# Two-layer graph network: third dense stage with one output of normalised rows and their root, last stage that gathers from it

## The chip, the cores and the metric

The kernel runs on one core of a Trainium2 chip. A core has five engines that work side by side: PE (matrix products; PEld is its weight load), DVE (vector), ACT (scalar, activations), POOL (general; it also issues indirect DMAs) and SP (issues DMAs), and 16 DMA engines that move data between HBM and the on-chip memory. The metric is device time in microseconds (us) of one execution; less is better.

## The reference

50,000 nodes with 256 features each, 12,500 edges sorted by destination. Cut to what matters:

```python
# first layer
e    = gelu((x[src] + edge_attr) @ W_pre + b_pre) * bases
y    = x + segment_sum(e, dst)
h    = relu(bn(y @ W1 + b1));  h = relu(bn(h @ W2 + b2))      # statistics over all nodes
x1   = layernorm(x + y + h)
# second layer
S    = x1[src]
m    = relu(relu(S @ W_rel[r].T + b_rel[r]) @ W_rel[r].T + b_rel[r])   # r = edge type
agg  = segment_sum(m, dst)
i, f, g, o = split(agg @ W_ih.T + b_ih + b_hh)
hn   = sigmoid(o) * tanh(sigmoid(i) * tanh(g))
z    = relu(relu(hn @ M1.T + b1) @ M2.T + b2) @ M3.T + b3
out  = layernorm(x1 + z)
```

A node that is no edge's destination has agg = 0, so its z is one constant row, `base`. Its output is layernorm(x1 + base).

## The kernel before

The program runs five stages one after another, each in a block of its own with a barrier behind it.

`edges0` computes the edge messages of the first layer, 25 blocks of 512 edges, while ACT's queue copies x to the scratch tensor y (25 pieces of 2 MB). After the last block it computes `base` and the bias rows of the second layer in one serial chain (lines 298 to 317 on PE, 358 to 366 on ACT, 444 to 482 on DVE). `dense1` adds the sums to y by indirect DMA and does the first product over 98 blocks of 512 nodes; `dense2` does the second.

`dense3` (line 871) goes over the 98 blocks of nodes once more. For block k: SP loads h2 and y (512 KB each; `load_h2`, `load_y`). ACT's `relu` makes r from h2. PE's `turn` transposes r into PSUM, eight times 128x128. DVE's `add` makes s = 2y + r; `row_stats` (line 857) and `bn_aggr` give mean and variance of each row. POOL's `deviations` (L1016 to L1027) turns variances into 1/root by a power. x1 = (s - mean) / root is made half on DVE (`normed`, L1059), half on ACT (`x1_part`, L1000). POOL's `add_base` (L1034) makes u = x1 + base, DVE takes its statistics too, and ACT's `normed` (L991) writes the normalised o. SP stores x1 and o, 512 KB each. The order on each engine is written out by hand in its `step(k, q)`: DVE does `add(k+3)`, statistics of u(k), `normed(k+1)`, statistics of s(k+3), `bn_aggr` of both; POOL `add_base(k+1)`, then `deviations` for s(k+3) and u(k) in one batch; ACT `x1_part(k+1)`, `relu(k+4)`, `normed(k-1)`. Engines run their instructions in order, and a wait holds up all that stands behind it on the same engine.

```python
def step(k, q):                        # ACT, L1004
    x1_part(k + 1, (q + 1) % 4)
    relu(k + 4, q)
    normed(k - 1, (q - 1) % 4)
```

`edges1` (line 1091) does the second layer for the 25 blocks of 512 edges. POOL fetches x1[src] and x1[dst] by indirect DMA, four of 128 rows to a block each (`fetch_src`, `fetch_dst`, L1190, L1200), and stores the new rows of a block into out (`store`, L1219, four). PE does the products in an order written out over k (L1310 on); in step k DVE makes u(k-1) and its statistics, POOL's `deviations(k-1)` follow. At its start SP loads the marks `cont` (1.6 MB) and `has` (3.2 MB), broadcast to all partitions.

Of the kernel before, what the change touches and what calls it, by code (L numbers as in the profile page):

```python
# [15 lines left out]
F = 256  # L16
C = F // P
# [9 lines left out]
COLS = 40  # L27
# [79 lines left out]
def edges0(nc, A, K, S):  # L107


    with ExitStack() as c:  # L110
# [5 lines left out]
        def sem(name):  # L116
# [10 lines left out]
        spare = [attr[:, (S.EB + n) % 4].rearrange("p c e -> p (c e)") for n in range(3)]  # L127
        raw_m = spare[0][:, 0:(NBLK - M1) * P].rearrange("p (n o) -> p n o", o=P)
        raw_rel = spare[1].rearrange("p (r c o) -> p r c o", r=2, c=C)
        rows = spare[2][0:4, 0:2 * F].rearrange("p (n f) -> p n f", n=2)  # L130
        spare_bases = bases[:, S.EB % 3].rearrange("p c e -> p (c e)")
        rows_h = spare_bases[0:4, 0:2 * F].rearrange("p (n f) -> p n f", n=2)
        rows_l = spare_bases[0:4, 2 * F:4 * F].rearrange("p (n f) -> p n f", n=2)
        wm_h, wm_l = sb("wm_h", [P, NBLK - M1, P], F32R), sb("wm_l", [P, NBLK - M1, P], F32R)
# [13 lines left out]
        hid_h, hid_l = sb("hid_h", [P, C, P], F32R), sb("hid_l", [P, C, P], F32R)  # L148
        a1, a1h, a1l = sb("a1", [P, P]), sb("a1h", [P, P], F32R), sb("a1l", [P, P], F32R)
# [8 lines left out]
        rel_i_full, has_done, has_kept, rel_full, bias_product = (  # L158
            sem("e0_rel_i_full"), sem("e0_has"), sem("e0_has_kept"), sem("e0_rel_full"), sem("e0_bias_product"))
# [9 lines left out]
        biases, cell_done, hid_done, gates_on, mlp_done, relu_done, product = (  # L169
            sem("e0_biases"), sem("e0_cell"), sem("e0_hid"), sem("e0_gates_on"), sem("e0_mlp"), sem("e0_relu"),  # L170
            sem("e0_product"))
        block = c.enter_context(nc.Block())
        EB = S.EB

        @block.sync
        def _(sp):
# [30 lines left out]
            sp.dma_start(K.b3[:], A["M_b3"].rearrange("(a f) -> a f", a=1).to_broadcast([P, F])).then_inc(wm_full, 16)  # L207
# [13 lines left out]
            sp.wait_ge(lo_done, EB - 3)  # L221
            sp.dma_start(raw_m, A["wt"][:, M1:NBLK]).then_inc(wm_full, 16)
            sp.wait_ge(lo_done, EB - 2)
            sp.dma_start(raw_rel.rearrange("p r c o -> p (r c o)"), A["wt"][:, REL:IH].rearrange("p b o -> p (b o)")).then_inc(rel_full, 16)
            sp.wait_ge(lo_done, EB - 1)
            sp.dma_start(rows, A["rows"]).then_inc(wm_full, 16)
# [30 lines left out]
        def _(pe):  # L257
# [29 lines left out]

            pe.wait_ge(consts, 1)
# [3 lines left out]
            for k in range(EB + 1):  # L292
                if k + 2 < EB:
                    turn(k + 2)
                if k < EB:
                    dense(k)
                if k >= 1:
                    back(k - 1)

            pe.wait_ge(gelu_done, EB)  # L300
            pe.wait_ge(rel_full, 16)
            pe.wait_ge(cols_full, 16)
            for r in range(2):
                for ic in range(C):
                    last = pe.matmul(pU[0:4, 1, r * F:(r + 1) * F], K.rel_b4[:, ic],
                                     raw_rel[:, r, ic], start=ic == 0, stop=ic == C - 1)
            last.then_inc(bias_product, 1)
            pe.wait_ge(mlp_done, 1)
            for ic in range(C):
                last = mm3(pe, pU[:, 0, 0:P], (wm_h[:, ic], wm_l[:, ic]), (hid_h[:, ic], hid_l[:, ic]), ic == 0, ic == C - 1)  # L310
            last.then_inc(product, 1)
            pe.wait_ge(mlp_done, 2)
            mm3(pe, pU[:, 0, 0:P], (wm_h[:, M2 - M1], wm_l[:, M2 - M1]), (a1h[:], a1l[:]), True, True).then_inc(product, 1)
            pe.wait_ge(mlp_done, 3)
            w3_h, w3_l = (w[:, M3 - M1:M3 - M1 + C].rearrange("p b o -> p (b o)") for w in (wm_h, wm_l))
            mm3(pe, pU[:, 0, 0:F], (a1h[:], a1l[:]), (w3_h, w3_l), True, True).then_inc(product, 1)

        @block.scalar
        def _(act):
# [37 lines left out]

            act.wait_ge(biases, 1)
            for n, func in ((0, ACT.Sigmoid), (1, ACT.Tanh), (2, ACT.Sigmoid)):
                act.activation(gate[:, n], K.gate_b[:, n * C:(n + 1) * C], func).then_inc(gates_on, 1)  # L360
            act.wait_ge(cell_done, 1)
            act.activation(cell_t[:], cell[:], ACT.Tanh).then_inc(gates_on, 1)
            act.wait_ge(product, 1)
            act.activation(a1[:], pU[:, 0, 0:P], ACT.Relu, bias=K.m_b[:, 0:1]).then_inc(relu_done, 1)
            act.wait_ge(product, 2)
            act.activation(a1[:], pU[:, 0, 0:P], ACT.Relu, bias=K.m_b[:, 1:2]).then_inc(relu_done, 1)

        @block.vector
        def _(dve):
# [36 lines left out]

            dve.wait_ge(run_full, 32)
# [9 lines left out]
            dve.wait_ge(consts, 5)  # L417
            dve.wait_ge(index_full, 48)
# [25 lines left out]

            dve.wait_ge(cols_full, 16)
            dve.tensor_tensor(out=K.gate_b[:], in0=K.cols[:, 0:GATES * C], in1=K.cols[:, GATES * C:2 * GATES * C],
                              op=ALU.add).then_inc(biases, 1)
            dve.wait_ge(wm_full, 48)
            then(dve.tensor_copy(wm_h[:], raw_m))
            then(dve.tensor_tensor(out=wm_l[:], in0=raw_m, in1=wm_h[:].bitcast(F32), op=ALU.subtract))  # L450
            dve.tensor_scalar(out=K.minus_rel_b[:], in0=K.rel_b, scalar1=-1.0, scalar2=None, op0=ALU.mult)
            dve.memset(K.ones[:].bitcast(F32), 1.0)
            then(dve.memset(K.rows[:].bitcast(F32), 0.0))
            then(dve.tensor_scalar(out=keep_l[:], in0=K.part[0:4], scalar1=2.0, scalar2=None, op0=ALU.is_ge))
            then(dve.tensor_scalar(out=keep_h[:], in0=K.part[0:4], scalar1=2.0, scalar2=None, op0=ALU.is_lt))
            then(dve.tensor_scalar(out=odd[:], in0=keep_l[:], scalar1=-2.0, scalar2=K.part[0:4, 0:1],
                                   op0=ALU.mult, op1=ALU.add))
            then(dve.tensor_scalar(out=even[:], in0=odd[:], scalar1=-1.0, scalar2=1.0, op0=ALU.mult, op1=ALU.add))
            dve.wait_ge(bias_product, 1)
            for r, mark in ((0, even), (1, odd)):  # L460
                then(dve.scalar_tensor_tensor(out=rows[:, 0], in0=pU[0:4, 1, r * F:(r + 1) * F], scalar=mark[:, 0:1],
                                              in1=rows[:, 0], op0=ALU.mult, op1=ALU.add))
            then(dve.tensor_copy(rows_h.bitcast(F32R), rows))
            then(dve.tensor_tensor(out=rows_l, in0=rows, in1=rows_h, op=ALU.subtract))
            then(dve.tensor_scalar(out=rows_l, in0=rows_l, scalar1=keep_l[:, 0:1], scalar2=None, op0=ALU.mult))
            for n in range(2):
                then(dve.scalar_tensor_tensor(out=K.rows[0:4, n], in0=rows_h[:, n], scalar=keep_h[:, 0:1],
                                              in1=rows_l[:, n], op0=ALU.mult, op1=ALU.add))
            dve.wait_ge(gates_on, 3)
            dve.tensor_tensor(out=cell[:], in0=gate[:, 0], in1=gate[:, 1], op=ALU.mult).then_inc(cell_done, 1)  # L470
            dve.wait_ge(gates_on, 4)
            dve.tensor_tensor(out=hid[:], in0=gate[:, 2], in1=cell_t[:], op=ALU.mult).then_inc(hid_done, 1)
            dve.wait_ge(hid_done, 1)
            wide = hid[:].rearrange("p (c o) -> p c o", o=1).to_broadcast([P, C, P])
            then(dve.tensor_copy(hid_h[:], wide))
            dve.tensor_tensor(out=hid_l[:], in0=wide, in1=hid_h[:].bitcast(F32), op=ALU.subtract).then_inc(mlp_done, 1)
            for n in range(2):
                dve.wait_ge(relu_done, n + 1)
                then(dve.tensor_copy(a1h[:], a1[:]))
                dve.tensor_tensor(out=a1l[:], in0=a1[:], in1=a1h[:].bitcast(F32), op=ALU.subtract).then_inc(mlp_done, 1)  # L480
            dve.wait_ge(product, 3)
            then(dve.tensor_tensor(out=K.base[:], in0=pU[:, 0, 0:F], in1=K.b3[:], op=ALU.add))
# [1153 lines left out]
```

## Time and profile before

| | |
|---|---|
| median of 3 runs | 2237.25 us (2236.58 to 2238.08) |
| profiled execution | 2248.79 us, of which its span is 2247.0 |
| `edges0` | 0 to about 302 us |
| `dense1` and `dense2` | about 304 to 1042 us |
| `dense3` | 1042 to 1582 us |
| `edges1` | 1583 to 2247 us |
| busy, whole span | PE 72%, DVE 74%, ACT 61%, POOL 58% |
| moved | 572.69 MB |

The page's second part cuts the span into 40 slices of 56 us; a digit is the busy share in tenths, and PEclk the clock granted to PE in tenths of full speed (2.4 GHz; 5 is 1.2 GHz). The stages are told apart by which engine is busy in them and by which lines the timeline shows. The profiled execution took 11.5 us more than the median of the timed runs.

### The profile page before, as it was taken

The page shows a single profiled execution, that of the slowest core. Times are in us where ns is not written, and L with a number is a line of the kernel's source. Part 1 is how long each engine was busy: PE and PEld are TensorE (multiplying, and loading weights), DVE is VectorE, ACT ScalarE, POOL GpSimd, SP SyncE. Part 2 cuts the span into 40 slices and gives each one's busy share as a digit, 9 for nine tenths or more (in the row PEclk, how much of TensorE's full clock was granted, in tenths as well). Part 3 has the DMA queues.
Part 4 walks back from the last instruction along what each step waited for, and adds up shares of the span by engine and source line. Part 5 has one row for each costly group of instructions (what it writes and reads, how often), then busy time and mean ns, then how long its engine had stood idle before and what let it go on. Part 6 is the DMA issues. An engine that isn't in the chain of part 4 may idle for free. (4 is left out here: it accounts for less than half of the span.)

```text
span 2247.0 us, 29418 instructions
## 1 busy us (share of the span) xinstructions
PE 1609.5 (72%) x7554; PEld 1295.5 (58%) x7554; DVE 1666.1 (74%) x3358; ACT 1365.9 (61%) x1981; POOL 1313.1 (58%) x1204
## 2 busy tenths in 40 slices
PE   2645569999996888994333333332599999999994
PEld 2434448888884655663232233232488778888884
DVE  2646646666667888996999999998377667777673
ACT  1322325555775766773888888887266656666663
POOL 5543147770006887001999999999446666666653
PEclk8877879999998999997555555555799999999997
DMA  9999759998879999995999999997412111212110
GB/s 341 368 347 352 260 161 340 342 340 316 289 249 285 342 339 342 344 325 232 385 397 399 401 404 400 395 407 308 169 37 67 63 62 57 65 63 64 55 53 32
DMA packets 171831, 572.69 MB, mean 255 GB/s; under 512 B 27441, under 2 KB 50583, under 8 KB 170322
## 3 DMA queue, kind: packets, MB, share of 16 engines
q1 hardware_dynamic: 123282, 445.99, 52.3%
q0 software_dynamic: 47136, 73.04, 13.8%
q10 hardware_dynamic: 1344, 52.84, 6.3%
q8 instruction: 31, 0.51, 0.1%
q14 instruction: 38, 0.31, 0.0%
HBM read 332.27 MB, written 295.04 MB: 279 GB/s over the span
## 5 line engine op out<-in xcount | busy, mean ns | idle before, releaser
L968 PE MATMUL d_pN<-k_ident,d_r 128*128 128x128 f32 x784 | 191.6, 425 | 337.2 <-ACT d_r L983 336.5
L968 PEld LDWEIGHTS d_pN<-k_ident,d_r 128*128 128x128 f32 x784 | 153.0, 222 | 375.9 <-issue 343.9
L500 DVE BATCH_NORM_STATS2 k_stats<-d_pH 128x512 f32 (+1 forms) x392 | 253.2, 688 | 100.8 <-PE d_pH L52 91.7
L991 ACT ACTIVATE d_o<-d_u,d_nb,d_rs 128x256 f32<-128x256 f32 x392 | 203.6, 590 | 81.2 <-POOL d_nb L1027 81.2
L1034 POOL TENSOR_TENSOR d_u<-d_x,k_base 128x1024 f32<-128x1024 f32 x98 | 230.9, 2356 | 14.6 <-DVE d_x L1059 9.5
L590 POOL DMA_INDIRECT scratch_y<-k_sums,k_target x98 | 151.9, 1550 | 120.7 <-POOLq L61 69.1
L50 PE MATMUL d_pH<-d_r_h,k_w_h 128*128 128x512 f32 x392 | 164.3, 419 | 57.3 <-DVE d_r_l L829 27.5
L780 ACT ACTIVATE d_r<-d_h,d_coef 128x512 f32<-128x512 f32 x196 | 149.2, 809 | 87.0 <-DVE d_r_l L829 41.8
L637 ACT ACTIVATE d_y_h<-d_pT 128x1024 fp32r<-128x1024 f32 x98 | 100.5, 1025 | 157.2 <-PE d_pT L606 133.1
L811 POOL DMA_INDIRECT scratch_y<-k_sums,k_target x98 | 175.0, 1786 | 33.3 <-issue 21.8
L530 POOL TENSOR_TENSOR bn_rstd<-bn_var,k_minus_half 128x2 f32<-128x2 f32 x2 | 1.5, 726 | 318.3 <-DMA d_h<-scratch_h 176.7
L237 POOL DMA_INDIRECT edge<-in_x,k_src x100 | 116.1, 1161 | 116.8 <-PE pT L264 89.7
L1025 POOL TENSOR_TENSOR d_rs<-d_v,k_minus_half 128x8 f32<-128x8 f32 (+1 forms) x101 | 166.2, 1645 | 8.4
L50 PE MATMUL d_pH<-d_y_h,k_w_h 128*128 128x512 f32 x392 | 163.4, 417 | 0.0
L676 DVE TENSOR_TENSOR d_y_l<-d_pT,d_y_h 128x1024 fp32r<-128x1024 f32 x98 | 120.0, 1225 | 57.7 <-ACT d_y_h L637 52.5
L983 ACT ACTIVATE d_r<-d_h,k_coef 128x512 f32<-128x512 f32 x196 | 147.5, 800 | 21.9 <-DMA d_h<-scratch_h 21.9
L1200 POOL DMA_INDIRECT e_xd<-scratch_x,k_dst_gather x98 | 144.6, 1476 | 26.6 <-issue 26.6
L52 PE MATMUL d_pH<-d_r_h,k_w_l 128*128 128x512 f32 x392 | 154.9, 395 | 0.0
L51 PE MATMUL d_pH<-d_r_l,k_w_h 128*128 128x512 f32 x392 | 154.4, 394 | 0.0
L52 PE MATMUL d_pH<-d_y_h,k_w_l 128*128 128x512 f32 x392 | 154.2, 393 | 0.0
L51 PE MATMUL d_pH<-d_y_l,k_w_h 128*128 128x512 f32 x392 | 153.3, 391 | 0.0
L1372 ACT ACTIVATE e_gate<-pG,k_gate_b 128x512 f32<-128x512 f32 (+1 forms) x150 | 99.1, 674 | 87.8 <-PE pG L52 65.1
(201 smaller groups left out, 4960.1 us busy)
## 6 DMA issues: line engine op xcount, KB each, us to landing
d_y<-scratch_y SPq DMA_DIRECT2D x196, 512.0 KB
scratch_h<-d_h SPq DMA_DIRECT2D x196, 512.0 KB
d_h<-scratch_h SPq DMA_DIRECT2D x196, 512.0 KB
scratch_y<-in_x ACTq DMA_DIRECT2D x25, 2000.0 KB
scratch_x<-d_x SPq DMA_DIRECT2D x97, 512.0 KB
out<-d_o SPq DMA_DIRECT2D x97, 512.0 KB, 7.7
attr<-in_attr_t SPq DMA_DIRECT2D x25, 512.0 KB, 28.4
bases<-in_bases_t SPq DMA_DIRECT2D x25, 512.0 KB
```

The lines of the kernel that those rows point to most:

```text
L50: pe.matmul(out, lhs[0], rhs[0], start=first, stop=False)
L51: pe.matmul(out, lhs[0], rhs[1], start=False, stop=False)
L52: return pe.matmul(out, lhs[1], rhs[0], start=False, stop=last)
L500: return dve.bn_stats(out, psum)
L590: pool.indirect_dma_start(out=A["y"], out_offset=bass.IndirectOffsetOnAxis(ap=K.target[:, t:t + 1], axis=0), in_=K.sums[:, t], in_offset=N ...
L780: last = act.activation(r[:, q % 2, cc], h1[:, q, cc * B:(cc + 1) * B], ACT.Relu, bias=coef[:, 1, cc:cc + 1], scale=coef[:, 0, cc:cc + 1])
L811: pool.indirect_dma_start(out=A["y"], out_offset=bass.IndirectOffsetOnAxis(ap=K.target[:, k:k + 1], axis=0), in_=K.sums[:, k], in_offset=N ...
L968: last = pe.transpose(pN[b][:, j, cc * P:(cc + 1) * P], r[:, b, cc, j * P:(j + 1) * P], K.ident[:])
L983: last = act.activation(r[:, q % 2, cc], h2[:, q, cc * B:(cc + 1) * B], ACT.Relu, bias=K.coef2[:, 1, cc:cc + 1], scale=K.coef2[:, 0, cc:cc ...
L991: last = act.activation(o[:, q, j], u[:, q, j], ACT.Identity, bias=nb[:, q, J + j:J + j + 1], scale=rs[:, q, J + j:J + j + 1])
L1025: pool.tensor_tensor(out=rs[:, q, now], in0=v[:, q, now], in1=K.minus_half[:, now], op=ALU.pow).then_inc(rs_done, 1)
L1034: pool.tensor_tensor(out=u[:, q], in0=x1[:, q], in1=wide, op=ALU.add).then_inc(u_done, 1)
```

## The change

`dense3` has one output for each block instead of two: rows of 260 columns, of which 256 are the normalised row and the next is its root sqrt(var + eps). x1 is not stored; it is root times the row, up to the mean of x1 + base, which is taken into the biases. The statistics of two rows come from one `bn_stats` over 512 elements read in turn from the two rows, with no `bn_aggr`. s is summed in PSUM by PE: a float32 product of y with twice the identity and eight products of r with the identity. DVE makes u = s / root + base out of PSUM, four rows of 256 columns. SP's store of block k follows the load of block k+7. ACT's order is new: `relu(0..3)`, then `normed(k)`, `relu(k+4)` for each k.

`edges1` gathers from out. Because its own stores overwrite rows that are still to be read as sources, blocks 0 to 3 of the sources are fetched directly, and blocks 4 to 24 are fetched in steps -1 to 5, three blocks a step, into `bounce`, moved out by SP to a scratch tensor and loaded from there later. Stores are held until step 6 (six buffers of o), then go three blocks a step until they have caught up. DVE multiplies source rows by their root (four instructions a block). `has` is loaded block by block. The chain at the end of `edges0` that makes `base` moves into its steps 5 to 10, with products of four columns, and its weights are loaded earlier.

```diff
 # edges0
-            sp.wait_ge(lo_done, EB - 3)
-            sp.dma_start(raw_m, A["wt"][:, M1:NBLK]).then_inc(wm_full, 16)
...
+                if SIDE <= k < SIDE + 5:
+                    base_mlp(k - SIDE)
...
+                if k == SIDE - 1:
+                    base_row()
+                if SIDE <= k < SIDE + 5:
+                    dve.wait_ge(side_product, k - SIDE + 1)
+                    (first_mlp, second_mlp, third_mlp, shifted_biases, bias_rows)[k - SIDE]()
 # dense3, SP
+            for k in range(NB + 3):
+                if k + 4 < NB:
+                    load(k + 4)
+                if k >= 3:
+                    store(k - 3)
 # dense3, PE
+            for k in range(NB):
+                pe.wait_ge(y_full[k % 4], 16 * (k // 4 + 1))
+                if k >= 4:
+                    pe.wait_ge(u_done, k - 3)
+                for two in range(J // 2):
+                    pe.matmul(pN[k % 4][:, 2 * two:2 * two + 2].rearrange("p j f -> p (j f)"), twice[:],
+                              y[:, k % 4, two * 2 * F:(two + 1) * 2 * F], start=True, stop=False)
                 pe.wait_ge(relu_done, k + 1)
-                wait(pe, s_done, k - 1)
                 for j in range(J):
                     for cc in range(C):
-                        last = pe.transpose(pN[b][:, j, cc * P:(cc + 1) * P], r[:, b, cc, j * P:(j + 1) * P], K.ident[:])
-                last.then_inc(turned, 1)
+                        last = pe.matmul(pN[k % 4][:, j, cc * P:(cc + 1) * P], r[:, k % 2, cc, j * P:(j + 1) * P], K.ident[:],
+                                         start=False, stop=j % 2 == 1 and cc == C - 1)
+                last.then_inc(summed, 1)
 # dense3, ACT
+            def normed(k):
+                n = (k - 1) % 4
+                act.wait_ge(nb_done, k + 1)
+                act.wait_ge(u_done, k + 1)
...
+            for k in range(4):
+                relu(k)
+            for k in range(NB):
+                normed(k)
+                if k + 4 < NB:
+                    relu(k + 4)
 # dense3, POOL
+            for n in range(-3, NB - 1):
+                a, b, at = n + 3, n + 1, n % 4
+                if real(a):
+                    pool.wait_ge(st1_done, a + 1)
+                if real(b):
+                    pool.wait_ge(st2_done, b + 1)
...
+                pool.tensor_scalar(out=v[:, at, now], in0=st[:, at, now, 2], scalar1=1.0 / F, scalar2=EPS,
+                                   op0=ALU.mult, op1=ALU.add).then_inc(v_done, 1)
...
+                pool.tensor_tensor(out=rs[:, at, now], in0=v[:, at, now], in1=K.minus_half[:, now], op=ALU.pow).then_inc(rs_done, 1)
...
+                    pool.tensor_tensor(out=nb[:, at], in0=nm[:, at], in1=rs[:, at, J:2 * J], op=ALU.mult).then_inc(nb_done, 1)
 # dense3, DVE
+            def pairs(out, rows):
+                for p in range(J // 2):
+                    last = dve.bn_stats(out[:, 2 * p:2 * p + 2].rearrange("p j s -> p (j s)"),
+                                        rows[:, 2 * p:2 * p + 2].rearrange("p j f -> p f j"))
...
+            def first(k):
+                dve.wait_ge(summed, k + 1)
...
+                pairs(st[:, (k - 3) % 4, 0:J], pN[k % 4]).then_inc(st1_done, 1)
+            def second(k):
+                dve.wait_ge(rs_done, batches(k - 3))
...
+                for j in range(J):
+                    last = dve.scalar_tensor_tensor(out=u[:, k % 3, j], in0=pN[k % 4][:, j], scalar=rs[:, (k - 3) % 4, j:j + 1],
+                                                    in1=K.base[:], op0=ALU.mult, op1=ALU.add)
...
+                pairs(st[:, (k - 1) % 4, J:2 * J], u[:, k % 3]).then_inc(st2_done, 1)
+            for k in range(-3, NB - 1):
+                if real(k + 3):
+                    first(k + 3)
+                if real(k + 1):
+                    second(k + 1)
 # edges1, POOL: order of a step
+                for n in now[0:1]:
+                    pick_src(n)
                 if real(k - 1):
                     deviations(k - 1)
                 if real(k + 1):
                     fetch_dst(k + 1)
-                if real(k - 1):
-                    store(k - 1)
-                if 2 <= k + 4 < EB:
-                    fetch_src(k + 4)
+                for n in now[1:]:
+                    pick_src(n)
...
+                if k >= HELD:
+                    for _ in range(3):
+                        if stored < min(k, EB):
+                            store(stored)
+                            stored += 1
 # edges1, DVE
+                    for j in range(tiles(k + 2)):
+                        row = xs[:, b, j]
+                        last = dve.tensor_scalar(out=row[:, 0:F], in0=row[:, 0:F], scalar1=row[:, F:F + 1], scalar2=None,
+                                                 op0=ALU.mult)
+                    last.then_inc(scaled, 1)
```

Here `rs_done` and `batches(n) = n + 4` count POOL's batches from n = -3; `nb_done` counts only batches with a block b, so `nb_done >= k + 1` is the batch n = k - 1.

## Rows read from the trace of the kernel before

**Rows 1.** Page, part 2: the span in 40 slices, busy and clock in tenths.
```profile
DVE  2646646666667888996999999998377667777673
PEclk8877879999998999997555555555799999999997
```

**Rows 2.** Windows: us; busy PE, PEld, DVE, ACT, POOL; clock; DMA share; GB/s.
```profile
800.00:900.00 100.00, 80.81 (x324) 58.44 (x323) 83.81 (x109) 68.70 (x82) 78.72 (x45) 1.00 1.09 342
1200.00:1300.00 100.00, 37.80 (x155) 29.87 (x153) 96.18 (x363) 85.52 (x154) 91.01 (x96) 0.50 1.02 400
2000.00:2100.00 100.00, 99.81 (x481) 83.54 (x479) 70.91 (x100) 62.16 (x92) 67.08 (x66) 1.00 0.21 65
```

**Rows 3.** Timeline, DVE, `dense3`: start, us, line, operation, tiles, count [idle before].
```profile
1300.86 1.18 DVE L1051 SCALAR_TENSOR_TENSOR d_s<-d_y,d_pN 128x1024 f32<-128x1024 f32 x1
1301.96 1.39 DVE L860 BATCH_NORM_STATS2 d_st<-d_u 128x6 f32<-128x256 f32 x4
1303.28 0.72 DVE L1059 TENSOR_SCALAR d_x<-d_s,d_mv,d_rs 128x256 f32<-128x256 f32 x2
1305.45 0.64 DVE L1081 BATCH_NORM_AGGREGATE d_mv<-d_st 128x2 f32<-128x6 f32 x8
1306.01 1.19 DVE L1051 SCALAR_TENSOR_TENSOR d_s<-d_y,d_pN 128x1024 f32<-128x1024 f32 x1
```

**Rows 4.** The same stretch, ACT.
```profile
1304.09 2.08 ACT L991 ACTIVATE d_o<-d_u,d_nb,d_rs 128x256 f32<-128x256 f32 x4 [0.91 <-POOL d_nb L1027]
1306.07 1.08 ACT L1000 ACTIVATE d_x<-d_s,d_nb,d_rs 128x256 f32<-128x256 f32 x2
1307.06 1.51 ACT L983 ACTIVATE d_r<-d_h,k_coef 128x512 f32<-128x512 f32 x2
```

**Rows 5.** The same stretch, POOL.
```profile
1301.44 0.24 POOL L1022 TENSOR_SCALAR d_nm<-d_mv 128x8 f32<-128x8 f32 x1
1302.07 1.67 POOL L1025 TENSOR_TENSOR d_rs<-d_v,k_minus_half 128x8 f32<-128x8 f32 x1
```

**Rows 6.** The same stretch, PE.
```profile
1303.31 1.96 PE L968 MATMUL d_pN<-k_ident,d_r 128*128 128x128 f32 x8 [3.30 <-ACT d_r L983]
```

**Rows 7.** Timeline, DVE: first block and last row statistics of `dense3`.
```profile
1055.34 1.22 DVE L1051 SCALAR_TENSOR_TENSOR d_s<-d_y,d_pN 128x1024 f32<-128x1024 f32 x1
...
1573.87 0.38 DVE L1081 BATCH_NORM_AGGREGATE d_mv<-d_st 128x2 f32<-128x6 f32 x4 [0.15 <-DVE d_st L860]
```

**Rows 8.** Timeline: statistics of 512 columns, float32 products, transposes at full clock.
```profile
287.19 3.58 PE L305 MATMUL pU<-attr,k_cols 128*4 128x256 f32 x8
...
324.19 1.30 DVE L500 BATCH_NORM_STATS2 k_stats<-d_pH 128x6 f32<-128x512 f32 x2 [0.59 <-PE d_pH L52]
...
2003.39 1.03 PE L1247 MATMUL pX<-k_ident,e_xs 128*128 128x128 f32 x8
```

**Rows 9.** Window inside those float32 products, columns as in Rows 2.
```profile
287.00:288.00 1.00, 1.00 (x5) 0.23 (x4) 0.96 (x2) 0.71 (x1) 0.00 (x0) 0.50 0.06 16
```

**Rows 10.** Timeline, end of `edges0`: DVE, ACT, DVE, POOL.
```profile
255.18 1.22 DVE L383 TENSOR_TENSOR attr<-pT,attr 128x1024 f32<-128x1024 f32 x1 [17.50 <-DMA attr<-in_attr_t]
...
287.29 1.02 ACT L342 ACTIVATE k_sums<-pS 128x1024 f32<-128x1024 f32 x1 [4.38 <-PE pS L285]
...
301.59 0.42 DVE L482 TENSOR_TENSOR k_base<-pU,k_b 128x256 f32<-128x256 f32 x1 [1.10 <-PE pU L52]
...
304.06 1.62 POOL L590 DMA_INDIRECT scratch_y<-k_sums,k_target  x1 [69.13 <-POOLq L61]
```

**Rows 11.** Timeline, PE: the first instruction of `edges1`.
```profile
1596.01 1.97 PE L1247 MATMUL pX<-k_ident,e_xs 128*128 128x128 f32 x8 [39.31 <-DMA e_xs<-scratch_x,k_src]
```

**Rows 12.** Groups by line, POOL, 1690 to 2170 us: count | busy us, mean ns.
```profile
L1200 POOL DMA_INDIRECT e_xd<-scratch_x,k_dst_gather x76 | 114.5, 1506 | 20.5 <-issue 20.5
L1219 POOL DMA_INDIRECT out<-e_o,k_target x80 | 84.0, 1050 | 24.4 <-issue 24.4
L1190 POOL DMA_INDIRECT e_xs<-scratch_x,k_src x74 | 79.6, 1076 | 22.6 <-issue 22.6
```

More of the change, by code:

```diff
@@ L16 @@
 F = 256
+FP = 260
 C = F // P
@@ L297, in _ @@
                 if k >= 1:
+                    if SIDE < k <= SIDE + 5:
+                        pe.wait_ge(side_ready, k - SIDE + 1)
                     back(k - 1)
[L300 to L316, printed above, removed]
+                if SIDE <= k < SIDE + 5:
+                    base_mlp(k - SIDE)
         @block.scalar
@@ new lines, in first_mlp, with second_mlp, third_mlp @@
+            def first_mlp():
+                dve.tensor_scalar(out=a1[:], in0=pS[:, 0, 0:4], scalar1=K.m_b[:, 0:1], scalar2=0.0,
+                                  op0=ALU.add, op1=ALU.max).then_inc(side_ready, 1)
+            def second_mlp():
+                dve.tensor_scalar(out=a2[:], in0=pS[:, 0, 0:1].to_broadcast([P, P]), scalar1=K.m_b[:, 1:2], scalar2=0.0,
+                                  op0=ALU.add, op1=ALU.max).then_inc(side_ready, 1)
+            def third_mlp():
+                then(dve.tensor_tensor(out=K.base[:], in0=pS[:, 0], in1=b3[:], op=ALU.add))
+                then(dve.bn_stats(base_st[:], K.base[:]))
+                then(dve.bn_aggr(base_mv[:], base_st[:]))
+                for oc in range(C):
+                    last = dve.tensor_scalar(out=base4[:, oc], in0=pS[:, 1, oc * 4:(oc + 1) * 4], scalar1=K.b3_col[:, oc:oc + 1],
+                                             scalar2=base_mv[:, 0:1], op0=ALU.add, op1=ALU.subtract)
+                last.then_inc(side_ready, 1)
@@ new lines, in shifted_biases @@
+            def shifted_biases():
+                moved = pS[:, 0, 0:2 * C * 4].rearrange("p (n o) -> p n o", o=4)[:, :, 0]
+                then(dve.tensor_tensor(out=K.minus_rel_b[:], in0=moved, in1=K.rel_b, op=ALU.subtract))
+                for r in range(2):
+                    for n in (r, r + 2):
+                        last = dve.tensor_scalar(out=b4[:, :, n], in0=K.minus_rel_b[:, r * C:(r + 1) * C], scalar1=-1.0,
+                                                 scalar2=None, op0=ALU.mult)
+                last.then_inc(side_ready, 1)
@@ L452, in _ @@
[L452 to L480, printed above, removed]
@@ L481, in _ @@
-            dve.wait_ge(product, 3)
-            then(dve.tensor_tensor(out=K.base[:], in0=pU[:, 0, 0:F], in1=K.b3[:], op=ALU.add))
+                if k == SIDE - 1:
+                    base_row()
+                if SIDE <= k < SIDE + 5:
+                    dve.wait_ge(side_product, k - SIDE + 1)
+                    (first_mlp, second_mlp, third_mlp, shifted_biases, bias_rows)[k - SIDE]()
 def node_rows(t, S):
@@ L854, in _ @@
             coef2_vector(dve)
-def row_stats(dve, stats, rows, done):
-    for j in range(J):
-        last = dve.bn_stats(stats[:, j], rows[:, j])
-    last.then_inc(done, 1)
-def row_moments(dve, mv, stats, past, done):
-    dve.sem_inc(past, 1)
-    for j in range(J):
-        last = dve.bn_aggr(mv[:, j], stats[:, j])
-    last.then_inc(done, 1)
 def dense3(nc, A, K, S):
@@ L1004, in step @@
-            def step(k, q):
-                if real(k + 1):
-                    x1_part(k + 1, (q + 1) % 4)
-                if real(k + 4):
-                    relu(k + 4, q)
-                if real(k - 1):
-                    normed(k - 1, (q - 1) % 4)
-            act.dma_start(raw_wl[:], A["wt"]).then_inc(K.wl_full, 16)
-            batch_steps(act, S.NB, step, 4)
+            act.dma_start(raw_wl[:], A["wt"]).then_inc(wl_full, 16)
+            for k in range(4):
+                relu(k)
@@ L1029, in add_base @@
-            def add_base(k, q):
-                pool.wait_ge(x1_done, k + 1)
-                pool.wait_ge(x1_rest, k + 1)
-                wait(pool, o_done, k - 3)
-                wide = K.base[:].rearrange("p (o f) -> p o f", o=1).to_broadcast([P, J, F])
-                pool.tensor_tensor(out=u[:, q], in0=x1[:, q], in1=wide, op=ALU.add).then_inc(u_done, 1)
-            def step(k, q):
-                if real(k + 1):
-                    add_base(k + 1, (q + 1) % 4)
-                if real(k + 3) or real(k):
-                    deviations(k, q)
@@ L1176, in _ @@
             sp.dma_start(cont[:], line.to_broadcast([P, S.TC * P])).then_inc(marks, 16)
[L1177 to L1179 removed]
+            load_has(2)
+            for k in range(-2, EB):
+                if k >= 1 and k + 3 < EB:
+                    load_src(k + 3)
+                if k >= 0 and k + 2 < EB:
+                    load_has_k(k + 2)
+                    if k + 3 < EB:
+                        load_has(k + 3)
+                for n in picks(k):
+                    move_out(n)
         @block.gpsimd
```

471 lines of the change are left out of this document (250 added, 221 removed).

## The prediction

> **What bounds the kernel now.** I read the slices of the page first, to see the stages by the busiest engine and by PE's clock [rows 1]; then one window in each of three stages [rows 2]; then the timeline of one step of `dense3`, engine by engine [rows 3 to 6]. The reader is to see three things. `dense3` runs with DVE at 96% and DMA at 400 GB/s, and PE, 38% busy, at half clock [rows 2]: 2.1 MB a block at 400 GB/s is 5.2 us, and DVE's step from one sum to the next is 5.15 us [rows 3], so two bounds lie together. `edges1` is PE's: 99.8% busy, DVE 71% [rows 2]. `edges0` waits for its loads near its end (17.5 us before the sum at 255) and closes with a serial chain in which no bulk transfer runs: the last sums are kept at 288.3, `base` is ready at 302.0, `dense1`'s first add starts at 304.06 [rows 10].
>
> **dense3, by throughput.** Bytes: 512 + 512 + 520 KB a block, 1.58 MB, 3.95 us at the 400 GB/s of [rows 2]. DVE: four statistics of 512 columns at 1.30 us the pair, 2.6 us [rows 8]; they replace eight of 256 (1.39 us for four [rows 3]), and `bn_aggr` (0.64) goes. The sum of 1024 columns (1.18) and the two scalings (0.72 for two, so the second starts 0.32 after the first) give way to four multiply-adds of 256, 1.36 us by that pitch [rows 3]. With one wait of DVE for itself (0.15 [rows 7]) that is 4.1 us. ACT: 1.98 + 1.51 = 3.5 us [rows 4], as `x1_part` (0.99) goes. POOL: `add_base` goes, 2.65 us from the first of its small operations to ACT's start stay [rows 4, 5]. PE: the eight products with the identity and the two with twice the identity have no row. The nearest is eight float32 products of 256 columns, 0.43 us each (3.58 less an end of about 0.15, by eight) at clock 0.50 [rows 8, 9], which is two clocks a column at 1.2 GHz. So y costs 2 x 0.85 = 1.7 us at that clock, and r 8 x 0.21 = 1.7, in line with the 1.96 that eight transposes take there [rows 6] and with 1.03 at full clock [rows 8]. Bounds for r: 1.03 below, 8 x 0.43 = 3.4 above (its weights have 128 columns, those of the row four). I take 1.96. By throughput alone the block would take 4.1 us, and 1.1 us a block would be won.
>
> **dense3, by its order.** I do not believe that number, because a loop of waits closes within two steps. DVE's step m is `first(m+3)`, then `second(m+1)`. Follow one block: `second(k)` ends step k-1. POOL's batch n = k-1 waits for it. ACT's `normed(k)` waits for that batch, and `relu(k+4)` stands behind `normed(k)` in ACT's queue. PE's r products of k+4 wait for `relu(k+4)`, and `first(k+4)` opens DVE's step k+1. Only step k lies between. The loop takes:
>
> - DVE step: 1.30 + 1.36 + 0.15 + 1.30 = 4.11 [rows 3, 7, 8]
> - to POOL 0.15 (priced as [rows 7]), POOL to ACT's start 1304.09 - 1301.44 = 2.65 [rows 4, 5]; the power stays eight wide, 1.67 of it
> - ACT `normed` 1.98, `relu` 1.51 [rows 4]
> - to PE 0.15, r products 1.96 at half clock [rows 6], to DVE 0.15
>
> That is 12.66 us for two steps, 6.3 us a step, against 5.15 now. Other loops are looser: y's products need only `second(k)`'s multiply-adds and fit into the 2.6 us and more that PE has left over at half clock (6.3 - 3.7); u has three buffers, which makes three steps; loads and stores have four blocks' time. The order of before holds the same loop over three steps: POOL's start at 1301.44, `normed`, `x1_part`, `relu` to 1308.57, then 0.15 and 1.96 give 1310.7 [rows 4 to 6]. With DVE's step and two hops that is 14.6 us, 4.9 a step, just under 5.15. It hid; with one step less it can't.
>
> PE's clock decides 0.47 us of this. PE would be busy for 3.7 of 6.3 us at half clock, 59%, with about 2.6 us idle in a piece. The rows have 38% at 0.50 and 81% at 1.00 [rows 2], so neither side is excluded. I take 0.50, as the work of this stage is next to the row of this stage.
>
> Sum for the stage. DVE's first block is at 1055.3 and its last `bn_aggr` ends at 1574.25 [rows 7]. After: the first four blocks go at PE's pace, 3.7 us, and step 0 ends at about 1055.3 + 11 + 4 = 1070. The other 96 steps take 96 x 6.3 = 605, to 1675. What follows (POOL, ACT, store) is as now. That is +101 us.
>
> **edges0.** The chain behind the last kept sums goes: from 288.3 to 304.06 stand 15.7 us, of which the barrier's 2.05 (302.01 to 304.06) stays, 13.7 us [rows 10]. Against it 0.85 MB of weights now load among the bulk loads, 2.4 us at 350 GB/s (`edges0` moves about what the 342 of [rows 2] shows). The moved steps wait in six blocks for each other (side products, small vector operations, two changes of the ACT table), some 20 us in total as an estimate from the chain's own 13.7 and its new hops; they are covered by the loads, for which DVE stalls 17.5 us at a time [rows 10]. Queued behind the waits are DVE's next sums and, through them, PE. If that cover is gone, up to 20 us come back. I take -11, range -14 to +6.
>
> **edges1.** PE starts at 1596, after the first sources, which share DMA with 4.8 MB of marks [rows 11]. Of these 2.8 MB come later, at most 7 us at 400 GB/s; the scaling of the sources (1.36 and a hop) goes in between. I take -3. In steady state DVE gains 1.36 us of scaling and 0.1 of multiply-adds and loses 0.5 of statistics and aggregation, with 29% free [rows 2]; PE has the same products. I cost it at nothing; were the cover gone, it would be 1 us a step, 24 us. POOL issues 16 DMAs in each of seven steps in place of 12: twelve at 1.08 + 0.30, four at 1.51 + 0.27, and 2.1 for `deviations` make 25.8 us [rows 5, 12], against a step of 24 us (80 stores in 480 us [rows 12]). Behind them wait `deviations` (needed by DVE a step later) and SP's moves. 7 x 1.8 = 13 us of lag meet some 10 us of lead: I take +2, range 0 to +30. The last stores are as now. Together -1.
>
> **Sum.** +101 - 11 - 1 = +89 us, against the profiled execution's 2248.8. That one lies 11.5 us above the median; the difference is applied to the median: 2237.25 + 89 = 2326 us.
>
> **Rivals.**
>
> 1. **PE at full clock in dense3.** r takes 1.03 in place of 1.96, the step 5.84: 96 x 0.47 = 45 us less, 2281. For it: real products, not transposes, and 59% busy. Against: 38% gave 0.50.
> 2. **The float32 products with 128 columns of weights cost double,** 3.4 for r: +1.5 on the loop, +72 us, 2398. [rows 8, 9] speak against it (two clocks a column, but with four columns of weights). The Trainium skill, "FP8 and Floating Point Precision", TensorE Precision Notes, says that true FP32 takes four passes through the array; by that each product would take 0.43 us and the time would be this rival's, while the row shows half of it.
> 3. **Statistics over two rows read in turn run at half rate,** 0.53 us more for each of four: +2.13 on the loop, +102 us, 2428. No row reads with such a stride, so the bound is open upwards. The Trainium skill, "SBUF — State Buffer", section "Door 1: The DMA port swizzle", says that an access that crosses to a new 16-byte line at each element pays a penalty; that would be this rival, and no row here shows it.
> 4. **POOL holds edges1 up.** If all sixteen issues cost 1.5 + 0.30, a step takes 30.9 us, 7 x 6.9 = 48 of lag less some 18 of lead: 28 us above the forecast, 2354.
> 5. **The loop does not bind, and the stage goes by throughput.** If ACT had `relu` far enough ahead, DVE's 4.1 us would be the step: 96 x 2.2 = 211 us less, 2115, faster than before. It decides from 5.2 us a step down: for that the loop would have to be 10.3 us and not 12.7. For it: ACT is only 55% busy by the sum, and bytes fall by a quarter. Against: `relu(k+4)` does stand behind `normed(k)`, and its pieces are measured.
>
> **How the numbers follow.** Forecast 0.47, rival 1 0.17, rival 4 0.10, rival 2 0.08, rival 3 0.10, rival 5 0.08. The range takes in the forecast and rivals 1, 2 and 4, with some 10 us for the small terms: 2268 to 2408. It leaves out 0.18. Only rival 5 is faster. Within 0.2% (4.5 us, about what a measurement of this kernel can tell from no change) lies no case, for mixtures 0.01. So faster 0.08, same 0.01, slower 0.91.
>
> **What would show it.** The step of `dense3`, from one `first` to the next, averages 6.3 us; DMA falls to about 250 GB/s and DVE to about 65% there; DVE waits before `first` for PE, PE before r for ACT's `relu`, ACT before `normed` for POOL. From the end of `second(k)` to the start of `first(k+4)` stand 8.5 us. `dense1` begins at about 293. Step times of 4.1 us, DVE or DMA at the brim, would prove me wrong; statistics of more than 0.7 us, or r products of more than 2.2, would make a rival right. In `edges1` PE stays above 97%.

## The result, and the profile after

The changed kernel takes 2398.68 us (median of 4 runs, 2397.45 to 2402.3) against 2237.58 for the kernel before beside it: 1.0723 times as long, 95% interval 1.0705 to 1.0742. That is 161 us slower, where 89 were forecast. The profiled execution took 2402.3 us with a span of 2400.5; all that follows compares it with the span of 2247.0 before, a difference of 153.5 us. The other 7.6 us are no loss that the profiles could show: the profiled execution before lies 11.2 us above its median, the one after 3.6.

Where the time went, by the same marks in both traces (us; for before, the starts in [rows 7, 10] and the two rows below):

| stretch | before | after | difference | forecast |
|---|---|---|---|---|
| start to first operation of `dense1` | 304.06 | 288.54 | -15.5 | -11 |
| from there to the first sum or statistic of `dense3` | 751.3 | 755.6 | +4.3 | 0 |
| `dense3` on DVE, first to last | 518.9 | 677.3 | +158.4 | +101 |
| to the first `e_xt_l` | 24.8 | 23.1 | -1.7 | -3 |
| `edges1`, from there to the last `e_u` | 629.9 | 638.9 | +9.0 | +2 |
| to the end | 18.1 | 17.2 | -0.9 | 0 |

The marks on DVE, kernel before (timeline: start, us, engine, line, operation, tiles, count [idle before]), first and last of `edges1`:

```profile
1599.07 1.23 DVE L1436 TENSOR_TENSOR e_xt_l<-pX,e_xt_h 128x1024 fp32r<-128x1024 f32 x1 [15.35 <-ACT e_xt_h L1344]
...
2228.94 0.69 DVE L1494 TENSOR_TENSOR e_u<-pM,e_xd 128x512 f32<-128x512 f32 x1 [2.16 <-issue]
```

The same of the changed kernel, with the first and the last statistics of `dense3`:

```profile
1044.09 1.30 DVE L1037 BATCH_NORM_STATS2 d_st<-d_pN 128x6 f32<-128x512 f32 x2 [2.23 <-PE d_pN L969]
...
1720.09 1.30 DVE L1037 BATCH_NORM_STATS2 d_st<-d_u 128x6 f32<-128x512 f32 x2
...
1744.47 1.23 DVE L1485 TENSOR_TENSOR e_xt_l<-pX,e_xt_h 128x1024 fp32r<-128x1024 f32 x1 [3.11 <-ACT e_xt_h L1391]
...
2383.35 0.87 DVE L1553 SCALAR_TENSOR_TENSOR e_u<-e_xd,pM 128x256 f32<-128x256 f32 x2 [2.17 <-PE pM L53]
```

The page of the changed kernel, part 2, the rows that answer to [rows 1]:

```profile
DVE  3674566666678889946556656655457687777873
...
PEclk8886799999989999968878878878689999999996
```

DVE's nines in `dense3` have become fives and sixes, and PE's clock, an even 5 before, is mostly 7 and 8 there. The windows (columns as in Rows 2) of `dense3` and `edges1`:

```profile
1200.00:1300.00 100.00, 68.30 (x289) 49.28 (x290) 57.86 (x112) 50.32 (x87) 34.99 (x73) 0.79 0.67 228
...
2000.00:2200.00 200.00, 200.00 (x957) 167.36 (x956) 156.71 (x214) 127.95 (x188) 105.83 (x103) 1.00 0.24 72
```

Nothing is at its brim in `dense3`: PE 68%, DVE 58%, ACT 50%, POOL 35%, 228 GB/s in place of 400. That is the look of a loop of waits. The page's groups show who waits for whom (count | busy us, mean ns | idle before, its main releaser):

```profile
L969 PE MATMUL d_pN<-k_ident,d_r 128*128 128x128 f32 x1568 | 268.9, 343 | 222.0 <-ACT d_r L980 222.0
...
L991 ACT ACTIVATE d_o<-d_u,d_nb,d_rs 128x256 f32<-128x256 f32 x392 | 203.2, 589 | 340.5 <-POOL d_nb L1026 340.4
...
L1037 DVE BATCH_NORM_STATS2 d_st<-d_pN 128x6 f32<-128x512 f32 x196 | 126.4, 687 | 272.2 <-PE d_pN L969 271.9
```

DVE waits for PE, PE for ACT, and ACT for POOL. That POOL waits for DVE closes the loop; this the profile does not name (it has "issue" ahead of L1018), but the kernel does (`st2_done`), and POOL starts 0.15 us after DVE's statistics end. One turn of it, on the timeline of the changed kernel (DVE, POOL, ACT and PE rows in order of time):

```profile
1301.89 1.29 DVE L1037 BATCH_NORM_STATS2 d_st<-d_pN 128x6 f32<-128x512 f32 x2 [5.41 <-PE d_pN L969]
...
1303.77 1.95 PE L969 MATMUL d_pN<-k_ident,d_r 128*128 128x128 f32 x16
...
1304.78 1.31 DVE L1037 BATCH_NORM_STATS2 d_st<-d_u 128x6 f32<-128x512 f32 x2
...
1305.55 1.88 PE L964 MATMUL d_pN<-d_y,d_twice 128*128 128x512 f32 x4
...
1306.01 1.28 DVE L1037 BATCH_NORM_STATS2 d_st<-d_pN 128x6 f32<-128x512 f32 x2
...
1306.24 0.20 POOL L1018 TENSOR_SCALAR d_v<-d_st 128x8 f32<-128x8 f32 x1 [7.04 <-issue]
...
1308.68 2.07 ACT L991 ACTIVATE d_o<-d_u,d_nb,d_rs 128x256 f32<-128x256 f32 x4 [6.12 <-POOL d_nb L1026]
...
1310.66 1.50 ACT L980 ACTIVATE d_r<-d_h,k_coef 128x512 f32<-128x512 f32 x2
...
1312.22 3.38 PE L969 MATMUL d_pN<-k_ident,d_r 128*128 128x128 f32 x16 [4.78 <-ACT d_r L980]
...
1315.63 1.30 DVE L1037 BATCH_NORM_STATS2 d_st<-d_pN 128x6 f32<-128x512 f32 x2 [5.45 <-PE d_pN L969]
```

`second` ends at 1306.09, POOL's batch starts 0.15 later, `normed` 2.44 after that, `relu` 1.98 later, r's products 1.56 later and take 3.38, and `first` opens the next step but one at 1315.63: 9.54 us, and with DVE's own step of 4.2 the 13.74 us from 1301.89 to 1315.63. Two steps go back to back, then DVE idles 5.4 us. That is the loop of the prediction, over two steps as foreseen. The turn shown has r's products at 3.38 us; over the 38 such turns read between 1100 and 1640 us they take 3.07 to 3.79, on average 3.57. What is new stands in the counts: r's eight products are **sixteen records**, y's two products four. A float32 product leaves two records here.

### The profile page after: what moved, and what is told of

Read it like the earlier page. It is cut to its first block and busy times, and to the rows that moved or that the text cites. A ratio compares the mean times of both kernels' runs of the same rounds, so it can differ in the third digit from the quotient of the medians.

```text
span 2400.5 us, 28831 instructions
## 1 busy us (share of the span) xinstructions
PE 1882.5 (78%) x8746; PEld 1483.1 (62%) x8746; DVE 1606.3 (67%) x2311; ACT 1274.3 (53%) x1785; POOL 1087.8 (45%) x1198
## 5 line engine op out<-in xcount | busy, mean ns | idle before, releaser
L969 PE MATMUL d_pN<-k_ident,d_r 128*128 128x128 f32 x1568 | 268.9, 343 | 222.0 <-ACT d_r L980 222.0
L969 PEld LDWEIGHTS d_pN<-k_ident,d_r 128*128 128x128 f32 x1568 | 256.1, 252 | 287.2 <-ACT d_r L980 261.5
L1037 DVE BATCH_NORM_STATS2 d_st<-d_pN 128x6 f32<-128x512 f32 x196 | 126.4, 687 | 272.2 <-PE d_pN L969 271.9
L964 PE MATMUL d_pN<-d_y,d_twice 128*128 128x512 f32 x392 | 208.6, 658 | 23.3 <-DMA d_y<-scratch_y 23.3
L1018 POOL TENSOR_SCALAR d_v<-d_st 128x8 f32<-128x8 f32 (+1 forms) x100 | 20.0, 200 | 441.8 <-issue 413.6
L1052 DVE SCALAR_TENSOR_TENSOR d_u<-d_pN,d_rs,k_base 128x256 f32<-128x256 f32 x392 | 161.0, 474 | 0.0
```

Source lines behind the costliest of these rows:

```text
L964: pe.matmul(pN[k % 4][:, 2 * two:2 * two + 2].rearrange("p j f -> p (j f)"), twice[:], y[:, k % 4, two * 2 * F:(two + 1) * 2 * F], start=T ...
L969: last = pe.matmul(pN[k % 4][:, j, cc * P:(cc + 1) * P], r[:, k % 2, cc, j * P:(j + 1) * P], K.ident[:], start=False, stop=j % 2 == 1 and ...
L1052: last = dve.scalar_tensor_tensor(out=u[:, k % 3, j], in0=pN[k % 4][:, j], scalar=rs[:, (k - 3) % 4, j:j + 1], in1=K.base[:], op0=ALU.mult ...
```

## The experiments

### Is it the loop, and over how many steps? (relu first)

```diff
             for k in range(NB):
-                normed(k)
                 if k + 4 < NB:
                     relu(k + 4)
+                normed(k)
```

> Against the changed kernel, only the order of two steps on ACT in dense3 differs: relu(k+4) stands ahead of normed(k). Theory (a loop of waits that closes within two of DVE's steps, 13.7 us measured, because relu stands behind normed): the loop now closes over three steps, 4.11 + 0.15 + 2.44 + 1.98 + 1.50 + 0.15 + 3.38 + 0.15 = 13.9 us for three, 4.6 us a step, or 4.2 if PE's clock rises to full (r 1.95); against 6.98 now that is 97 x 2.4 to 97 x 2.8, so 2130 to 2170 us in all, DVE about 95% busy in the stage. Rival (PE's own work bounds the step: eight r products and two y products at half clock would take 3.4 + 3.4 = 6.8 us): nothing changes, 2400 us. A second rival (1.58 MB a block, if the stage could move no more than the 230 GB/s seen): 6.9 us a step, 2400 us.

Measured: 2131.66 us (2128.75 to 2135.76), 0.9534 of the kernel before (0.9517 to 0.955), so 267 us below the changed kernel and 105 below the kernel before. `dense3` takes 410.7 us in place of 677.3. Its window, columns as above:

```profile
1200.00:1300.00 100.00, 91.06 (x488) 59.71 (x487) 99.13 (x195) 84.05 (x145) 58.10 (x122) 1.00 1.01 383
```

DVE is 99% busy with a step of 4.1 us, and 383 GB/s flow. The same products, bytes and statistics run in 0.6 of the time, so neither PE's work nor the transfers held the changed kernel. Two steps on ACT in the other order did. Part of the gain is PE's clock, 1.00 here and 0.79 there: the kernel with y twice (below) has the old order at 1.00, and its `dense3` takes 609.5 us. As an estimate from these, 68 of the 267 us come with the clock and some 199 with the loop's third step.

### One piece of the loop longer, one shorter (power twice, half of r)

```diff
...
+                pool.tensor_tensor(out=more[:, at, now], in0=v[:, at, now], in1=K.minus_half[:, now], op=ALU.pow)
                 pool.tensor_tensor(out=rs[:, at, now], in0=v[:, at, now], in1=K.minus_half[:, now], op=ALU.pow).then_inc(rs_done, 1)
```

> The changed kernel with one more power of the same size on POOL in each batch of dense3, into a tile that nobody reads (1.64 us in the trace). Theory (POOL's batch lies on the loop, and the loop closes within two steps): +1.64 us on 13.74, +0.82 us a step, 97 x 0.82 = +80 us, 2480 us. Rival (PE's work or the transfers bound the step; POOL has 4 of 7 us free): no change, 2400 us. If the loop closed within one step it would be +159, within three +53.

Measured: 2482.42 us, `dense3` 760.4, +83.1. That is 0.85 us for each of 98 blocks, where half of the 1.64 added is 0.82; a loop of one step would give 1.64, of three 0.55. The small rest is not settled: r's products where they bind are 3.74 us long on average here, 0.17 more than before, which alone would be 0.08 a block. POOL, 35% busy, passed half of its added time on: the share that a loop over two steps gives.

```diff
                 for j in range(J):
-                    for cc in range(C):
+                    for cc in range(1):
                         last = pe.matmul(pN[k % 4][:, j, cc * P:(cc + 1) * P], r[:, k % 2, cc, j * P:(j + 1) * P], K.ident[:],
-                                         start=False, stop=j % 2 == 1 and cc == C - 1)
+                                         start=False, stop=j % 2 == 1)
```

This kernel leaves out the second half of r, so its output is not the reference's.

> The changed kernel without the four of eight r products of a block that carry the second half of the features (so the sum lacks r there); all else stays. Theory (r's products are 3.4 us of the two-step loop): -1.7 us on the loop, -0.85 us a step, 97 x 0.85 = -82 us, 2318 us. Rival (PE's work bounds the step): -1.7 us a step, -165 us, 2235 us. If r's products were not on the loop: 2400 us.

Measured: 2313.87 us, `dense3` 602.2, -75.1, 0.77 us a block. A turn that binds has, on PE in this kernel:

```profile
1310.92 1.88 PE L969 MATMUL d_pN<-k_ident,d_r 128*128 128x128 f32 x8 [4.11 <-ACT d_r L980]
```

Over the turns from 1100 to 1640 us the r products that bind take 2.04 us on average, against 3.57 in the changed kernel: 1.53 less, half of it 0.77. The product is on the loop with its full length, and PE's total work isn't what counts (that would have been -1.7 a step).

### The clock of the product on the loop (y twice)

```diff
+                for two in range(J // 2):
+                    pe.matmul(pN[k % 4][:, 2 * two:2 * two + 2].rearrange("p j f -> p (j f)"), twice[:],
+                              y[:, k % 4, two * 2 * F:(two + 1) * 2 * F], start=True, stop=True)
                 for two in range(J // 2):
```

> The changed kernel with the two products of y issued twice in each block of dense3 (each first pair is a closed sum of its own that the second overwrites, so the result is the same): more work for PE, placed where PE waits for ACT's relu. Theory (a loop of two steps, with r's eight products on it at the granted clock; y's products lie beside it): if the added work brings the clock from half during r to full, r takes 1.95 in place of 3.38, -0.72 us a step, about -70 us, 2330 us. If the clock stays at half, PE has 3.4 + 2 x 3.4 = 10.2 us of work a step and the time is about 2700 us. Rival (PE's work bounds the step now): longer in either case, by 97 x 1.7 = 165 us at full clock, 2565 us, or more.

Measured: 2378.43 us, 48 above the theory's 2330 and far below the rival's 2565. Its `dense3` took 609.5 us, 67.8 less than in the changed kernel. Most of the rest lay in `edges1` (678.6 in place of 638.9), and two other kernels on the same chip had the same (below). So it ran again beside the changed kernel:

> The changed kernel with y's products issued twice in dense3, once more beside the changed kernel on one chip. Its dense3 took 609.5 us from the first statistics to the last in place of 677.3. Theory: 68 us less than the changed kernel here, with PE's clock at 1.00 in the stage. Rival (the stage's gain is given back in edges1, as its first run of 2378 us could be read): 20 to 25 us less only.

Measured: 2365.83 against 2432.67 us, -66.8, `dense3` 609.5 against 676.5. A window of `dense3` in this last run:

```profile
1200.00:1300.00 100.00, 86.56 (x392) 52.29 (x392) 66.55 (x128) 55.74 (x96) 39.12 (x81) 1.00 0.75 255
```

And the r products that bind, on its timeline:

```profile
1311.34 2.05 PE L972 MATMUL d_pN<-k_ident,d_r 128*128 128x128 f32 x16 [1.62 <-ACT d_r L983]
```

More work made the kernel faster. In the changed kernel PE idles 4.78 us ahead of the r products that bind, and as they start the clock falls. Windows of 1 us there, columns as above:

```profile
1311.00:1312.00 1.00, 0.00 (x0) 0.00 (x0) 0.00 (x0) 1.00 (x2) 1.00 (x1) 1.00 0.44 166
1312.00:1313.00 1.00, 0.78 (x5) 0.79 (x6) 0.00 (x0) 0.32 (x2) 0.88 (x3) 0.85 0.89 362
1313.00:1314.00 1.00, 1.00 (x7) 1.00 (x6) 0.00 (x0) 1.00 (x3) 0.00 (x0) 0.50 0.71 160
...
1316.00:1317.00 1.00, 1.00 (x3) 0.38 (x2) 1.00 (x3) 0.32 (x1) 0.00 (x0) 0.95 0.50 45
```

So these 3.38 us are for the most part, not all, at 1.2 GHz; in turns where the clock has fallen before they start (below, after 4.14 us of idle, in a second trace of the changed kernel) they take 3.78:

```profile
1305.02 3.78 PE L969 MATMUL d_pN<-k_ident,d_r 128*128 128x128 f32 x16 [4.14 <-ACT d_r L980]
```

The r products of the other block of the pair, which follow work, take 1.95. With the gap filled the clock stays at 2.4 GHz (1.00) and both take about 2.05.

### The loop after the repair (relu first, power twice)

The edits of the first and second experiment together.

> The kernel with relu(k+4) ahead of normed(k) and with one more power on POOL in each batch of dense3 (1.64 us, into a tile that nobody reads). There DVE is 99% busy with a step of 4.14 us, and ACT waits 0.65 us a step for POOL. Theory (the loop now closes over three steps and is 12.5 us with r at full clock, just under 3 x 4.14): 12.5 + 1.64 = 14.2 us for three, 4.7 us a step, +0.6 a step, +58 us on 2132, so 2190; if the clock falls to half as PE gets gaps, r adds 1.4 us, 5.2 a step, 2235. Rival A (the loop was broken for good, DVE alone is the bound): no change, 2132. Rival B (the loop still closes over two steps and r's clock alone made it short): 14.1 us for two, 7.1 a step, 2415.

Measured: 2233.35 us, `dense3` 464.5, +53.8 on relu first's 410.7: 0.55 us a block, a third of 1.64. Both rivals fall. DVE now waits for PE once in three steps:

```profile
1303.63 1.30 DVE L1039 BATCH_NORM_STATS2 d_st<-d_pN 128x6 f32<-128x512 f32 x2 [1.31 <-PE d_pN L970]
...
1317.66 1.30 DVE L1039 BATCH_NORM_STATS2 d_st<-d_pN 128x6 f32<-128x512 f32 x2 [1.30 <-PE d_pN L970]
```

Three steps take 14.03 us, 4.68 each. So the repaired order has the loop over three steps, and only just: 14.03 less 1.64 is 12.4 us, as much as three of DVE's 4.14. Its whole time is above the expected 2190 for the same reason as y twice's: `edges1` took 684.5 us there, 640.8 in relu first.

### What three kernels had in edges1, and a better order there (changed again, best)

```diff
-                if real(k + 2):
-                    b = (k + 2) % 4
+                for m in {-2: (0, 1), -1: ()}.get(k, (k + 2,)):
...
-                for n in now[0:1]:
-                    pick_src(n)
+                if k < HELD - 1:
+                    for n in now[0:1]:
+                        pick_src(n)
                 if real(k - 1):
                     deviations(k - 1)
+                if k >= HELD - 1:
+                    for n in now[0:1]:
+                        pick_src(n)
```

> The kernel with relu(k+4) ahead of normed(k) in dense3, and two changes of order in edges1: DVE scales the sources of blocks 0 and 1 together before the first step (block 1's scaling stands behind two subtractions now, and PE waits 4.5 us for it); in the last step with three picks POOL computes the deviations before the first pick (it comes to them 8.5 us after the statistics are ready, and one step of edges1 takes 29.2 in place of 24.5 us there). Theory (both waits are on PE's path in a stage that PE bounds): -4 and -4 us against relu first alone, so 2124 us. Rival (POOL's 26 us a step of issues is what counts, whatever their order; and the gap of PE at the start only moves): 2131 us, as with relu first alone.

Measured: 2165.14 us, above relu first's 2131.66, on another chip, where the kernel before took 2248.49 and not 2236.23. Of its `edges1` 84.8 us lie between the first `e_xt_l` and the first `e_u`, 58.0 in relu first. So all went to one chip together:

> The changed kernel itself once more, on the same chip as the three that follow, since three kernels run on one chip (y twice, relu first with a power more, best) each had about 27 us more in the first 60 us of edges1 than four run on another, in waits of ACT ahead of its first e_msg whose releaser the profile does not name. If those 27 us belong to the chip and not to the kernels: the same number here as in the other kernels of this call; if they come from the kernels' own changes, 2400 us here.

> As before it, and in edges1 the sources of blocks 0 and 1 scaled together, and the deviations ahead of the first pick in the last step with picks. Theory (both waits are on PE's path): 8 us less than relu first on the same chip. Rival (only the order of waits changes): the same within 2 us.

Measured there: the changed kernel 2432.67 us, with 83.8 us in that stretch (57.5 before), so the 26 us are the chip's, not the experiments'. Some 11 us more lie in the steps behind it (`edges1` 675.7 in all, 638.9 on the first chip). ACT in the changed kernel on that chip:

```profile
1757.65 1.03 ACT L1391 ACTIVATE e_xt_h<-pX 128x1024 fp32r<-128x1024 f32 x1 [7.32 <-remote]
1775.29 0.60 ACT L1405 ACTIVATE e_msg<-pM 128x512 f32<-128x512 f32 x1 [16.61 <-remote]
1785.90 0.60 ACT L1405 ACTIVATE e_msg<-pM 128x512 f32<-128x512 f32 x1 [10.01 <-remote]
```

On the first chip the same rows wait 4.59, 3.64 and 2.37 us for PE. The profile names no releaser; what it is stays open. Three of the four chips that the experiments ran on showed it, in every kernel that holds the new `edges1`; the kernel before was only 10 to 12 us longer on them than on the fourth.

Best and relu first, side by side: 2161.72 us (2157.8 to 2178.16) and 2173.73 (2165.14 to 2181.06), ratios to the kernel before 0.9625 (0.9598 to 0.9652) and 0.9654 (0.9633 to 0.9675). These overlap. The two side by side on one more chip:

> The same with the two changes of order in edges1. Theory: without the stall both waits of PE (4.5 us for the scaling of block 1, about 4 us for the late deviations) are on its path, 8 us less than relu first; rival: no difference beyond 2 us, the 12 us between the medians on the other chip being scatter.

Measured: 2158.8 us, 0.962 (0.9594 to 0.9646), against 2169.13, 0.9668 (0.9642 to 0.9693). Twice 10 to 12 us less, near the 8 expected, each time with intervals that touch: likely a gain, not a settled one. Which of the two edits gave it is not shown. PE's wait for the scaled sources (4.73 and 4.33 us) is gone with the scaling moved, but the stretch to the first `e_u` is 84.7 us with it and 82.8 without on one chip, 81.9 and 88.7 on the other; ACT's wait behind it stays and varies by more than the gain. Best ran on no chip without that wait. The fastest time of all is relu first's, 2131.66.

## Why the prediction was right, and by what it was off

- **The loop over two steps: right.** Each piece but one came as foreseen: DVE's step 4.12 to 4.2 (4.11), to POOL 0.15 (0.15), POOL to ACT 2.44 (2.65), `normed` and `relu` 1.98 and 1.56 to the next start (1.98 and 1.66). The runs show it as a loop, by +83 us for a power, -75 for half of r, and -267 for the order (some 68 of it with the clock).
- **The length of r's products: the term that was mis-sized,** 3.57 us on average where it binds, not 1.96. It is 1.61 us on the loop, 0.805 a step, 98 x 0.805 = 79 us. The step that failed was "The nearest is eight float32 products of 256 columns, 0.43 us each". [Rows 8] show eight records of L305, but that line stands in two nested loops of two: four products of 0.85 us, so four clocks a column at 1.2 GHz. With 128 weight columns it is the same: 3.78 us for 1024 columns and 2.08 for the 512 of half of r, both wholly at half clock, leave 1.70 for 512, 4.0 clocks each. Rival 2 named the right price for a wrong reason (128 columns of weights against 4). The eight transposes of [rows 6], 1.96, which I leaned on as the nearest row, are one record each at half of that cost. The y products were mis-sized in the same way (1.7 us forecast at half clock, 1.88 measured at full), but they lie beside the loop. Counting the instructions of a line in the code against the count of its row would have shown it. The Trainium skill ("FP8 and Floating Point Precision", TensorE Precision Notes) says that true FP32 takes four passes through the array. The traces agree, with these 4.0 clocks a column; the prediction had set it aside for a misread row.
- **The clock: 0.50 was nearly right where it counted** and wrong on average (0.79 in the window above, 0.83 from 1080 to 1600 us). Rival 1 (2281) did not come. It would have needed both: y twice, with r at 2.05, is the kernel that the forecast described, and its `dense3` of 609.5 us stands beside the 620 forecast for 1.96.
- **Why +158 and not +180:** with 3.57 for r the loop of the forecast is 14.3 us; two steps took 13.8 (677.3 over 49). In the turn shown POOL to ACT is 0.21 shorter than foreseen, `relu` with its hop to PE 0.10, the hop to DVE 0.12, DVE's step 0.09 longer.
- **Statistics read with a stride (rival 3): no loss.** 687 ns a piece on `pN`, which lies in PSUM, and 693 on `u` in SBUF; the contiguous 512 columns of `dense1` and `dense2` took 690 in the same trace. The Trainium skill ("SBUF — State Buffer", "Door 1: The DMA port swizzle") gives a penalty for an access that crosses to a new 16-byte line. It does not show in the statistics of `u`, 693 ns against 690.
- **edges0: the mechanism right.** `dense1` starts at 288.54 (293 foreseen): the last kept sums came 1.5 us earlier (286.8, 288.3), not later, and the 13.7 us chain is gone with nothing in its place. The size is known only roughly: with the same `edges0` the experiments start `dense1` at 282.1 to 295.3. Of the 15.5 us 4.3 were lost again ahead of `dense3`'s first statistics: 2.2 as DVE now waits for PE at its first block, the [2.23 <-PE] in the marks above, and 2.1 in `dense1` and `dense2`. The stretch takes 750.3 to 755.6 us in the traces with the same code, so a difference of 4.3 is within its scatter.
- **edges1: +6.4 with its ends, not -1.** I costed the scaling of the sources "at nothing"; at the start it has no cover. From the first `e_xt_l` to the first `e_u` stand 57.5 us, 50.3 before. That is 7.2 us; all the rest of the stage adds 1.8. The steady steps are 24.5 us. One step takes 29.2, where POOL comes late, as rival 4 had it; it costs 4.7 us, not 28 (with sixteen issues POOL's `deviations` at 1887.43 and 1914.31 are 26.9 us apart, 25.8 forecast). No experiment separates this step from the rest. Changed kernel, DVE's statistics, POOL's use of them, ACT's wait for it, and DVE and PE behind:

```profile
1877.55 1.32 DVE L1559 BATCH_NORM_STATS2 e_st<-e_u 128x6 f32<-128x512 f32 x2
...
1887.43 0.25 POOL L1236 TENSOR_SCALAR e_nm<-e_st 128x4 f32<-128x4 f32 x1
...
1889.37 2.08 ACT L1447 ACTIVATE e_o<-e_u,e_nb,e_rs 128x256 f32<-128x256 f32 x4 [4.11 <-POOL e_nb L1242]
...
1892.02 2.46 DVE L1501 TENSOR_TENSOR_SCAN e_msg<-e_cont,e_msg 128x512 f32<-128x512 uint8 x2 [5.50 <-ACT e_msg L1405]
...
1895.12 0.50 PE L51 MATMUL pG<-e_m1p_h,k_wl_h 128*128 128x512 f32 x1 [2.85 <-DVE e_m1p_l L1485]
```

- **Rival 5 (throughput) was one exchange away.** Its 2115 us and 4.1 us a step are what relu first shows (2132, 4.14), for the reason it gave: `relu` far enough ahead on ACT. The judgement that `relu(k+4)` stands behind `normed(k)` decided the sign.

The median came 73 us above the forecast, inside its range only because rival 2 lay in it. That rival 2's 2398 us is the measured median is luck in part: its term came out larger, the loop's other pieces shorter, `edges0` better and `edges1` worse than its sum has them.

## What to carry to other kernels

Write down the loop of waits with the number of steps it spans: where it is longer than every engine's own work, its length over that number is the step, however idle the engines look, and a piece added to it costs its length by that number (here a half, then a third). Before sizing a piece by a row, count the instructions of its line in the code against the row's count. Where an engine serves two blocks in turn, put the work that opens a later block ahead of the work that closes the present one.

## What the runs showed of the hardware that I had not expected

- A float32 product leaves two records and takes four clocks a column, with 4 weight columns as with 128 (3.58 us for four of 256 columns; 3.78 for eight of 128 and 2.08 for four, all at 1.2 GHz); a float32 transpose one record and half of that.
- PE's clock can fall between two blocks of one stage. The kernels in which PE idled 4 to 7 us ahead of every second block (changed, half of r, power twice) show 0.76 to 0.83 from 1080 to 1600 us, those in which PE waited at most 2.5 us there (power twice after the repair, y twice, relu first) 1.00 from 1080 to 1440, and useless products put into the gap were worth 67 us.
- The start of the new `edges1` depends on the chip: 57 to 58 us in the first traces, 82 to 89 on three other chips, in waits whose releaser the profile does not name.
